# The small embedding tables of a recommendation kernel padded to 128 rows, and the dense features turned later

## What is computed

```python
e = stack([tbl_0[ids[:, 0]], ..., tbl_25[ids[:, 25]]], axis=1)      # 512 x 26 x 128
combined = concatenate([dense[:, None, :], e], axis=1)              # 27 vectors a sample
interactions = einsum('bfd,bgd->bfg', combined, combined)
z = concatenate([dense, interactions[:, iu, ju]], axis=1)           # 351 pairs
h = concatenate([z, dense], axis=1)                                 # 607
h = maximum(h @ W_top1 + b_top1, 0)                                 # 512
h = maximum(h @ W_top2 + b_top2, 0)                                 # 256
y = h @ W_top3                                                      # 1
```

## Time and profile before

| | us |
|---|---|
| median of three runs | 136.37 (136.06 to 137.54) |
| the profiled execution, its own time | 135.71 |
| its span, first to last instruction | 133.9 |
| mean granted PE clock, share of full | 0.987 |

### The profile page before, as it was taken

How to read it: one execution, slowest core, us unless ns; L and a number is a source line. 1 busy time by engine, 2 the same in 40 slices (tenths; PEclk the granted TensorE clock), 3 DMA queues, 4 the chain that set the end, 5 groups by cost and what they waited for, 6 DMA issues and landing times.

```text
span 133.9 us, 2251 instructions
## 1 busy us (share of the span) xinstructions
PE 105.2 (79%) x772; PEld 94.9 (71%) x772; DVE 78.5 (59%) x199; ACT 70.3 (52%) x211; POOL 83.1 (62%) x92
## 2 busy tenths in 40 slices
PE   0000559959179799897699999999999997979994
PEld 0000427738067587787599999899998997969992
DVE  6005076867165879199999487479479728095001
ACT  3030165692473984398656098445376751547222
POOL 3278787887778778787787787787777773000000
PEclk9999999999967999999999999999999999999999
DMA  2895654899975442121221221221221221000000
GB/s 46 252 258 183 179 194 151 261 271 258 259 177 162 159 127 64 39 59 39 59 62 40 59 62 45 54 59 48 55 58 43 61 62 40 0 0 5 0 0 0
DMA packets 6041, 13.23 MB, mean 99 GB/s; under 512 B 1823, under 2 KB 2848, under 8 KB 5902
## 3 DMA queue, kind: packets, MB, share of 16 engines
q1 hardware_dynamic: 2668, 7.06, 17.6%
q0 software_dynamic: 2560, 5.25, 15.3%
q10 hardware_dynamic: 802, 0.78, 2.0%
HBM read 13.08 MB, written 0.00 MB: 98 GB/s over the span
## 4 chain that ended last, share of the span: by engine, by line
PE 58%; DMA 18%; SPq 12%; DVE 6%; issue 2%; ACT 2%; DVEq 0%; ACTq 0%
PE gram_ps L484 19%; DMA table_sb<-in_tbl 18%; PE dense_ps L499 14%; SPq L202 9%; PE turn_ps L458 5%; PE dense_ps L508 4%; PE turn_ps L499 4%; PE gram_ps L542 3%; SPq L204 3%; PE gram_ps L544 3%; DVE pairs L425 3%; DVE features_t L166 2%; PE dense_ps L491 2%; PE gram_ps L593 1%; PE dense_ps L516 1%
## 5 line engine op out<-in xcount | busy, mean ns | idle before, releaser
L234 POOL DMA_INDIRECT rows<-in_gathered_tables,row_at x80 | 81.9, 1023 | 28.3 <-issue 24.1
L314 ACT COPY pairs<-gram_ps 27x56 f32<-27x56 f32 (+1 forms) x128 | 31.8, 249 | 15.7 <-PE gram_ps L484 14.3
L425 DVE COPY pairs<-gram_ps 27x56 f32<-27x56 f32 (+1 forms) x128 | 32.6, 254 | 7.9 <-PE gram_ps L484 5.9
L484 PE MATMUL gram_ps<-features_t 128*123 128x108 f32 x256 | 30.3, 272 | 4.1 <-DVE pairs L425 1.9
L484 PEld LDWEIGHTS gram_ps<-features_t 128*123 128x123 f32 x256 | 28.8, 187 | 5.4 <-issue 5.4
L542 PE MATMUL gram_ps<-one_hot,table_hi 125*128 125x512 f32 x48 | 22.5, 468 | 7.8 <-ACT one_hot L267 6.2
L166 DVE COPY features_t<-turn_ps 128x512 f32<-128x512 f32 x16 | 17.1, 1066 | 15.9 <-PE turn_ps L458 15.7
L544 PE MATMUL gram_ps<-one_hot,table_lo 125*128 125x512 f32 x48 | 21.1, 439 | 0.0
L499 PE MATMUL dense_ps<-pairs,w_pairs_sb 128*128 128x128 f32 x168 | 20.8, 275 | 0.0
L499 PEld LDWEIGHTS dense_ps<-pairs,w_pairs_sb 128*128 128x128 f32 x168 | 19.7, 192 | 0.1
L542 PEld LDWEIGHTS gram_ps<-one_hot,table_hi 125*128 125x128 f32 x48 | 10.6, 220 | 12.3 <-ACT one_hot L267 7.9
(11 more groups left out here) (43 smaller groups left out, 66.1 us busy)
## 6 DMA issues: line engine op xcount, KB each, us to landing
table_sb<-in_tbl SPq DMA_DIRECT2D x5, 500.0 KB
w_pairs_sb<-in_w_pairs SPq DMA_DIRECT2D x1, 1792.0 KB, 14.8
hot_ids_sb<-in_hot_ids SPq DMA_DIRECT2D x6, 256.0 KB
rows<-in_gathered_tables,row_at POOLq DMA_INDIRECT x80, 2.7
w_dense_sb<-in_w_dense SPq DMA_DIRECT2D x1, 512.0 KB, 17.1
w_sb<-in_w SPq DMA_DIRECT2D x1, 512.0 KB, 24.6
table_sb<-in_tbl ACTq DMA_DIRECT2D x1, 500.0 KB
dense_rows<-in_dense ACTq DMA_DIRECT2D x1, 256.0 KB, 13.6
```

Source lines behind the costliest of these rows:

```text
L234: pool.indirect_dma_start(rows[:, u, m, :], None, gathered_tables, bass.IndirectOffsetOnAxis(ap=row_at[:, u, m:m + 1], axis=0)).then_inc(r ...
L314: last = act.copy(*pair_block(u, j, k))
L425: last = nc.vector.tensor_copy(*pair_block(u, j, k))
L484: last = nc.tensor.matmul(gram_ps[0:quad_rows, u % 2, q, 0:4 * FEATURES], flat_features[:, b * SLOTS:b * SLOTS + quad_rows], features_t[:, ...
```

## The change

The six hot tables are laid in one array of 128 x 6 x 1024 floats: each is padded with 24 rows of zeros to 1024 rows, so that it is 128 partitions of 8 rows. The kernel takes `hot_rows` as 128 and `hot_parts` as 8 for each; the number of products, one-hots and copies stays what it was, on 128 partitions where it was 125. Each table is still one transfer of its own on the queue it had, in the same order, now of 512 KB with 4 KB a partition (and 24 KB from one partition's piece to the next in memory).

The four transposes of the dense features are moved on PE from before the first table to behind the first table's 16 products. ACT's copy of them is moved from between `high_part(0)` and `high_part(1)` to behind the first one-hot of table 1, and has a semaphore of its own, `dense_copied`; the counts of `whole_made` are one less everywhere. SP's loop of two steps is written out.

```diff
-    hot_rows = [next(r for r in range(P, 0, -1) if table.shape[0] % r == 0) for table in hot_tables]
-    hot_parts = [table.shape[0] // r for table, r in zip(hot_tables, hot_rows)]
-    max_parts = max(hot_parts)
+    max_parts = hot_tables.shape[2] // dim
+    hot_rows, hot_parts = [P] * n_hot, [max_parts] * n_hot
...
                     if n > 0:
-                        sp.dma_start(table_sb[0:hot_rows[n], n, 0:hot_parts[n] * dim],
-                                     table.rearrange("(p c) d -> p (c d)", c=hot_parts[n])).then_inc(hot_in[n], 16)
+                        sp.dma_start(table_sb[:, n, :], hot_tables[:, n, :]).then_inc(hot_in[n], 16)
...
-                with sp.Fori(0, tiles - 2) as t:
+                for t in range(tiles - 2):
...
-                act.dma_start(table_sb[0:hot_rows[0], 0, 0:hot_parts[0] * dim],
-                              hot_tables[0].rearrange("(p c) d -> p (c d)", c=hot_parts[0])).then_inc(hot_in[0], 16)
+                act.dma_start(table_sb[:, 0, :], hot_tables[:, 0, :]).then_inc(hot_in[0], 16)
...
                 high_part(0)
-                act.wait_ge(dense_turned, 1)
-                nc.scalar.activation(whole_t[:, 0, :], turn_ps[:, 0, :], ACT.Copy).then_inc(whole_made, 1)
                 high_part(1)
...
                     one_hot_part(share[0])
+                    if n == 1:
+                        act.wait_ge(dense_turned, 1)
+                        nc.scalar.activation(whole_t[:, 0, :], turn_ps[:, 0, :], ACT.Copy).then_inc(dense_copied, 1)
...
-                dve.wait_ge(whole_made, n_hot)
+                dve.wait_ge(dense_copied, 1)
+                dve.wait_ge(whole_made, n_hot - 1)
                 nc.vector.tensor_copy(slots[:, 0:n_hot, :], whole_t[:, 0:n_hot, 0:P]).then_inc(whole_placed, 1)
...
-                pe.wait_ge(ident_made, 1)
-                pe.wait_ge(dense_in, 16)
-                for t in range(tiles):
-                    last = nc.tensor.transpose(turn_ps[:, 0, t * P:(t + 1) * P], dense_rows[:, t, :], ident[:, :])
-                last.then_inc(dense_turned, 1)
...
+                    if c == hot_parts[n] - 1 and n == 0:
+                        pe.wait_ge(ident_made, 1)
+                        pe.wait_ge(dense_in, 16)
+                        for t in range(tiles):
+                            last = nc.tensor.transpose(turn_ps[:, 0, t * P:(t + 1) * P], dense_rows[:, t, :], ident[:, :])
+                        last.then_inc(dense_turned, 1)
...
+    hot_tables = _np.zeros((len(HOT), 128, -(-max(tables[i].shape[0] for i in HOT) // 128), dim), w1.dtype)
+    for n, i in enumerate(HOT):
+        hot_tables[n].reshape(-1, dim)[:tables[i].shape[0]] = tables[i]
+    hot_tables = hot_tables.reshape(len(HOT), 128, -1).transpose(1, 0, 2)
```

More of the change, by code:

```diff
@@ L131, in dlrm_program @@
         one_hot_used, whole_made, dense_turned = sem("one_hot_used"), sem("whole_made"), sem("dense_turned")
+        dense_copied = sem("dense_copied")
         rows_in = [[sem(f"rows_in{at}_{n}") for n in range(n_groups)] for at in range(tiles * units)]
@@ L200, in _ @@
                 sp.dma_start(ids_sb[:, :, :], ids).then_inc(ids_in, 16)
-                for n, table in enumerate(hot_tables):
+                for n in range(n_hot):
                     sp.dma_start(hot_ids_sb[:, n, :], hot_ids[n:n + 1, :].broadcast_to([P, batch])).then_inc(hot_in[n], 16)
                     if n > 0:
-                        sp.dma_start(table_sb[0:hot_rows[n], n, 0:hot_parts[n] * dim],
-                                     table.rearrange("(p c) d -> p (c d)", c=hot_parts[n])).then_inc(hot_in[n], 16)
+                        sp.dma_start(table_sb[:, n, :], hot_tables[:, n, :]).then_inc(hot_in[n], 16)
                 sp.dma_start(w_dense_sb[:, :, :], w_dense.rearrange("c p n -> p c n")).then_inc(weights_in, 16)
@@ L208, in _ @@
                 sp.dma_start(w2_sb[:, :, :], w2.rearrange("(c p) n -> p c n", p=P)).then_inc(weights_in, 16)
-                with sp.Fori(0, tiles - 2) as t:
+                for t in range(tiles - 2):
                     sp.wait_ge(y_out, t + 1)
-                    sp.dma_start(y_line[:, bass.ds(t * P, P)], y_row[0:1, bass.ds(t * P, P)]).then_inc(y_stored, 16)
+                    sp.dma_start(y_line[:, t * P:(t + 1) * P], y_row[0:1, t * P:(t + 1) * P]).then_inc(y_stored, 16)
                 sp.wait_ge(y_out, tiles)
@@ L415, in _ @@
                 nc.vector.tensor_tensor(w_dense_sum[:, :], w_dense_sb[:, 0, :], w_dense_sb[:, 1, :], ALU.add).then_inc(w_dense_summed, 1)
+                dve.wait_ge(dense_copied, 1)
+                dve.wait_ge(whole_made, n_hot - 1)
+                nc.vector.tensor_copy(slots[:, 0:n_hot, :], whole_t[:, 0:n_hot, 0:P]).then_inc(whole_placed, 1)
                 dve.wait_ge(whole_made, n_hot)
-                nc.vector.tensor_copy(slots[:, 0:n_hot, :], whole_t[:, 0:n_hot, 0:P]).then_inc(whole_placed, 1)
-                dve.wait_ge(whole_made, 1 + n_hot)
                 def other_pairs(u):
@@ L475, in products @@
                     if u < 2:
-                        pe.wait_ge(whole_made, n_hot + u)
+                        pe.wait_ge(whole_made, n_hot - 1 + u)
                     else:
@@ L528, in _ @@
                     if c == 0 and n >= 2:
-                        pe.wait_ge(whole_made, n)
+                        pe.wait_ge(whole_made, n - 1)
                     if c == 0:
@@ L545, in _ @@
                                      one_hot[0:r, i % ring, :], start=False, stop=(c == hot_parts[n] - 1)).then_inc(one_hot_used, 1)
+                    if c == hot_parts[n] - 1 and n == 0:
[4 more added lines that the diff above has]
+                        last.then_inc(dense_turned, 1)
                     if c == hot_parts[n] - 1 and n in EARLY:
                         if n == EARLY[0]:
-                            pe.wait_ge(whole_made, 1)
+                            pe.wait_ge(dense_copied, 1)
                         transpose_unit(EARLY.index(n))
@@ L641 @@
         give("hot_ids", ids.T[list(HOT)]),
-        [give(f"tbl_{i}", tables[i]) for i in HOT],
+        give("hot_tables", hot_tables),
         give("dense", inputs["r_dense_features"]),
```

## The result

The changed kernel takes 132.58 us (median of four runs, 132.26 to 133.03); the kernel before took 136.95 in the four runs now at hand (136.06 to 138.34). The ratio is 0.970, with a 95% interval of 0.962 to 0.979. In the profiled executions the span falls from 133.9 to 131.2 us and the time from 135.71 to 133.03: 2.7 us each, and this is the difference that the traces can explain. The forecast was 3.0.

A forecast was written before the change was run, and what follows sets the result against it. Table arrival sets the pace up to 42 us, with POOL's gathers a second chain; -3.3 (slack at unit 13) + 0.2 (ids) + 0.1 (bytes, waits) = -3.0 us, from 136.37 to 133.4 us, range 131.2 to 135.8.

The forecast's parts named there:

- Loads on a third of the engines: Small-table loads: 125 partitions use 5 of 16 DMA engines, about a third; 128 partitions use all 16.
- When the tables land: Table loads at the start: last table there at about 25 us (27 at worst), not 42.3.
- The lookups' end: First pair products, after the table lookups: at 44 us instead of 54.49, 10.5 us earlier; bounds 40 and 48.
- The slack at unit 13: Main loop, where PE needs gather 70: only 3.3 of the 10.5 us gained earlier reach the end.
- The dense turn: Dense features' transposes on PE, moved behind table 0: worth 0 alone; lets PE begin at about 8 us, not 15.
- The clock rival: PE idling before units 12 or 13 lowers its clock, costing 1.7 us each time: 135.1 to 136.8 us; 14%.
- The starving gathers: Gathers wait between loads on full DMA engines; POOL's stream ends 8 us late, 4.7 us slower, 141 us; 6%.
- Ids late by 1.0 and stretches of 7 us: Slow end of the forecast case: late gather start and longer early gather issues leave a 1.6 us gain, 134.8 us.
- rival (3): Early gathers' stretched issue goes with the loads; POOL's stream ends up to 5.9 us sooner, 127.9 us; 5%.

The follow-up runs named there:

- the ids alone ahead: Changed kernel, but SP and ACT issue their other loads only once the ids have landed: 130.65 us, ratio 0.958 to the kernel before.

## Why the prediction was right

- **Loads on a third of the engines.** Held: 125 partitions in one transfer give a busy share of 0.59 in 8 to 24 us, 125 and 3 give 0.57, and 128, or 112 and 13, give 1.03 to 1.05. The counts 5 and 16 are the rule of the Trainium skill, "DMA: Bandwidth & Descriptors", in the section on why a DMA increments its semaphore by 16. The runs bear it out by these shares and by the loads that are late again with 125 and 3, not by a count of engines.
- **When the tables land.** Mis-sized, without effect. "23 us" stood on 265 GB/s for full engines; they moved 405. The load of the last table, issued at 6.94 us, landed 11.8 later, at 18.7 and not at 25, and the weights were in by 27. From table 2 on no high half waited for a load; the last was made at 28.26.
- **The lookups' end**, forecast 44 and bounded by 40 and 48: 44.75. The wait named for it, that of unit 3 for gather 20, was there, and that its size came out is partly luck: the gather was issued at 35.87 us and not at 33.25, since its early stretches came sooner, and landed in 2.6 us and not in 4.8 to 7.6, since the loads were done by then. PE turned its rows at 38.52, within the 38 to 41 of the forecast. The first product was forecast at 8 and came at 9.87, since DVE's first one-hots follow both low halves of table 0.
- **The slack at unit 13**, forecast 3.3 us: the wait is there, and the term came out at 2.7, which is 3.3 less 0.43 (the later gather 70) and 0.14 (from landing to turning). The difference is mostly the stream. Its start was forecast 0.2 later and was 0.42 earlier; its stretches were forecast unchanged and rose by 0.84, to about 6.9 us for the first 44, just within the bound of 7. Gather 70 was issued at 98.92 and not 98.49, and PE turned its rows 0.14 us after they landed.
- **The dense turn**, forecast 0: no difference at the first product where the loads are fast.
- **The clock rival.** PE was idle 1.58 us before unit 3's rows and 0.60 more before the fifth, and the granted clock was 0.74 and 0.50 in 38 to 42 us, the lower level. It fell on table 5's products, which the wait for unit 5 at 50 us covers. With the ids alone ahead PE didn't wait there, its clock stayed at 1.00, and from the last turned row of unit 3 to the pair products it took 4.3 us and not 5.9: the lower level cost 1.6 us of the lookups. Behind that wait it was 0.83 over 50 to 60 us, again ahead of waits that cover it. From 60 us on it was 1.00: the waits at units 12 and 13 (1.20 and 0.80 us) left it at its upper level, and the case didn't come.
- **The starving gathers.** Landing took 5.7 to 6.9 us in the full stretch, under the 7.3 to 8.2 seen before, and late gathers landed in 2.5 again.
- **Two of its sums.** Ids late by 1.0 and stretches of 7 us leave 3.3 - 1.0 - 1.1 - 0.1 = 1.1 us and not 1.6, so that case ends at 135.3 and not 134.8; rival (3), 9.2 less 0.3, gives 8.9 and not 8.5. Neither enters the forecast.

The medians fell by more than the traces say (4.4 us against 2.7): the kernel before ranges over 2.3 us in its runs, and its profiled execution (135.71) lies under all of them, while that of the changed kernel (133.03) is the slowest of its four. Beside the 136.0 to 136.1 that the kernel before took in 20 more runs on two chips, the gain is 3.4 to 3.6 us.

## What to carry to other kernels

When a transfer is slow, look at the DMA share while it alone is in flight: here a share of 0.40 to 0.47 while ACT waited meant that the shape of the transfer, and not the memory, was the limit, and three partitions of padding, or a cut into 112 and 13, mended it. Before pricing such a gain, find the stream that nothing in the change moves and read its distance to the consumer at several places; that distance (here 3 us of 10) is the gain, and what remains afterwards is to be had at the start of that stream, which cost two waits here.

## What was not expected

Full engines are not one rate. In 8 to 24 us the changed kernel moves 405 GB/s at a DMA share of 1.03 (with the dense turn first 406, with the ids alone 396), while the 112 and 13 partitions of separate tables move 255 at 1.05, on the same chip as the 406. The same run with 112 and 13 moves 377 and 398 GB/s in 26 to 28 and 28 to 30 us, when by the order of the queue the weights are what is left, so the lower rate isn't one of that run or chip. The two kernels differ in the array, whose 4 KB pieces lie 24 KB apart, in the zeros and in the number of transfers; which of these it is was not tried.
